# Routed blocks of a mixture-of-experts layer: the high half of the activations turned by DMA in odd blocks

## The reference, cut to what matters

```
logits = x @ router_w ; the 2 best of 8 experts per token, softmax over the two
for each expert e and each token routed to it:
    g, u = split(x @ w1[e])            # 256 -> 2 x 512
    y   += score * (silu(g) * u) @ w2[e]   # 512 -> 256
y += (silu(x @ w_gate) * (x @ w_up)) @ w_down   # shared expert, all tokens
```

## Time and profile before

| | us |
|---|---|
| median of 3 runs (lowest, highest) | 351.46 (351.23, 351.64) |
| span of the profiled execution | 350.0 |
| PE busy in it | 340.2 (97%) |
| DVE, ACT, POOL busy | 235.3 (67%), 214.1 (61%), 197.2 (56%) |
| mean granted PE clock | 0.996 of full |

### The profile page before, as it was taken

How to read it: one execution, slowest core, us unless ns; L and a number is a source line. 1 busy time by engine, 2 the same in 40 slices (tenths; PEclk the granted TensorE clock), 3 DMA queues, 4 the chain that set the end, 5 groups by cost and what they waited for, 6 DMA issues and landing times.

```text
span 350.0 us, 9157 instructions
## 1 busy us (share of the span) xinstructions
PE 340.2 (97%) x2926; PEld 257.0 (73%) x2926; DVE 235.3 (67%) x585; ACT 214.1 (61%) x389; POOL 197.2 (56%) x293
## 2 busy tenths in 40 slices
PE   7999999999999999999999999999999999999994
PEld 7878878888888898888988465656556556666663
DVE  4999989899888887978788554463544543333441
ACT  3678959796877987746536444455545444554452
POOL 4777568786876768565356444353443355344635
PEclk9999999999999999999999999999999999999998
DMA  6992152554875555735765439659677866876761
GB/s 192 391 357 40 33 125 59 125 145 161 198 201 93 151 163 140 214 109 133 250 233 134 108 61 116 92 84 98 80 103 94 95 99 86 98 109 102 88 65 22
DMA packets 76108, 45.90 MB, mean 131 GB/s; under 512 B 59936, under 2 KB 71200, under 8 KB 75680
## 3 DMA queue, kind: packets, MB, share of 16 engines
q1 hardware_dynamic: 62000, 34.82, 41.0%
q0 software_dynamic: 9392, 10.44, 19.4%
q10 hardware_dynamic: 4672, 0.07, 1.2%
HBM read 19.09 MB, written 12.97 MB: 92 GB/s over the span
## 4 chain that ended last, share of the span: by engine, by line
PE 72%; DVE 13%; issue 5%; ACT 4%; DMA 3%; SPq 1%; POOL 1%; DVEq 0%; POOLq 0%; ACTq 0%
PE bU L1124 13%; PE bG L1124 13%; PE bV L1149 7%; PE bQ L1149 6%; PE bU L239 6%; PE bG L239 5%; PE bD L1001 5%; DVE ab L1626 3%; PE bK L1104 3%; PE bV L239 2%; PE bQ L239 2%; DMA xT<-rows 2%; PE bK L239 2%; DVE st L1493 1%; PE bT L891 1%
## 5 line engine op out<-in xcount | busy, mean ns | idle before, releaser
L1626 DVE SCALAR_TENSOR_TENSOR ab<-bU,sg 128x512 f32<-128x512 f32 x64 | 44.1, 689 | 66.3 <-PE bU L1124 52.7
L800 POOL DMA_INDIRECT out_y<-xs,dst_row x32 | 50.6, 1580 | 55.8 <-DMA out_y<-xs,dst_row 26.2
L1278 ACT ACTIVATE sg<-bG 128x512 f32<-128x512 f32 x64 | 38.0, 594 | 43.8 <-PE bG L1124 26.7
L1124 PE MATMUL bG<-we,work 128*128 (+1 forms) x216 | 52.6, 380 | 0.0
L575 POOL DMA_INDIRECT x_rows<-rows,slot_u x32 | 42.0, 1313 | 18.8 <-issue 14.3
L1124 PE MATMUL bU<-we,work 128*128 (+1 forms) x216 | 52.6, 379 | 0.0
L1443 ACT ACTIVATE ws_h<-ab 128x512 f16<-128x512 f32 x36 | 22.7, 630 | 41.5 <-DVE ab L1626 41.5
L1948 DVE TENSOR_TENSOR ws_h<-ab,ws_h 128x512 f16<-128x512 f32 x36 | 24.9, 693 | 20.8 <-ACT ws_h L1443 20.8
L1285 ACT ACTIVATE ah<-ab 128x512 f16<-128x512 f32 x32 | 20.1, 629 | 28.6 <-DVE ab L1626 28.5
L1124 PEld LDWEIGHTS bG<-we,work 128*128 128x128 f16 (+1 forms) x216 | 20.7, 99 | 19.3 <-issue 1.6
L1124 PEld LDWEIGHTS bU<-we,work 128*128 128x128 f16 (+1 forms) x216 | 19.8, 99 | 17.4
(11 more groups left out here) (348 smaller groups left out, 820.0 us busy)
## 6 DMA issues: line engine op xcount, KB each, us to landing
stage<-in_w_expert SPq DMA_DIRECT2D x24, 512.0 KB, 5.0
we<-in_w_shared SPq DMA_DIRECT2D x3, 1024.0 KB, 11.5
out_y<-xs SPq DMA_DIRECT2D x8, 256.0 KB, 2.6
xs<-bo POOLq DMA_DIRECT2D x7, 256.0 KB, 4.6
xs<-in_x SPq DMA_DIRECT2D x1, 1280.0 KB, 18.0
x_rows<-we SPq DMA_DIRECT2D x9, 134.0 KB
xs<-in_x SPq DMA_DIRECT2D x3, 256.0 KB, 4.1
work<-x_rows SPq DMA_TRANSPOSE x40, 2.9
```

The source lines that it names most:

```text
L800: pool.indirect_dma_start(out_rows, bass.IndirectOffsetOnAxis(ap=dst_row[:, b:b + 1], axis=0), ya[b % NY], None, bounds_check=NT * P - 1, ...
L1124: ins = pe.matmul(dst[t * n:(t + 1) * n, :], x2[:, hi * KC + k, t * n:(t + 1) * n], w[t][lo][:, k, half, :], start=s == 0 and k == 0, stop ...
L1278: act.activation(sg[q][:], src[:], ACT.Silu, scale=1.0 / WS).then_inc(S["sg_done"], 1)
L1626: dve.scalar_tensor_tensor(out=ab[q][:], in0=src[:], scalar=1.0 / WS, in1=sg[q][:], op0=ALU.mult, op1=ALU.mult).then_inc(S["a_done"], 1)
```

## The change

In odd blocks up to 33 (17 of the 36 blocks) the high half is no longer turned on PE and copied by ACT: SP issues a transposing DMA for it (`turn_whole`), in the same step and just ahead of the one for the low half, as soon as `ar_h` is written. `expert_down` of an odd block waits for that DMA, and the counts of the semaphores of the remaining PE turns are adapted (`on_pe`). Even blocks and the last two blocks stay as they were. On POOL, the hold counts are read with a load that also asserts their bounds, each to a value of its own, instead of a plain load to one of two registers.

```diff
+        def by_dma(b):
+            return b % 2 == 1 and b < NBLK - 1
+        def on_pe(b):
+            return sum(not by_dma(n) for n in range(b + 1))
+        def high_in(b):
+            return S[f"ath_in{b % NA}"], 16 * sum(by_dma(n) for n in range(b % NA, b + 1, NA))
...
+            def turn_whole(b):
+                n = b % NA
+                sp.wait_ge(S["ah_done"], NP * B + b + 1)
+                if b >= NA:
+                    sp.wait_ge(S["o_ps"], b - NA + 1)
+                sp.dma_start_transpose(aT_h[n], ar_h[n]).then_inc(S[f"ath_in{n}"], 16)
...
             for b in range(NBLK):
+                if by_dma(b):
+                    turn_whole(b)
                 if b < NBLK - 1:
                     turn_low(b)
...
-            hold_reg = [pool.alloc_register(f"hold_reg{q}") for q in range(2)]
-            last_hold_reg = pool.alloc_register("last_hold_reg")
+            hold = {}
...
             def load_hold(b):
                 row = HALF if b - 1 in MIXED else 0
-                pool.reg_load(hold_reg[b % 2], hold_i[row:row + 1, b:b + 1])
+                hold[b] = pool.value_load(hold_i[row:row + 1, b:b + 1], min_val=16, max_val=16 * NBLK)
...
                 if b == NBLK - 2:
-                    pool.reg_load(last_hold_reg, hold_i[0:1, NBLK:NBLK + 1])
+                    hold[NBLK] = pool.value_load(hold_i[0:1, NBLK:NBLK + 1], min_val=16, max_val=16 * NBLK)
...
             def turn_high(b):
                 pe.wait_ge(S["ah_done"], NP * B + b + 1)
                 if b >= 1:
-                    pe.wait_ge(S["ath_done"], b)
+                    pe.wait_ge(S["ath_done"], on_pe(b) - 1)
...
             def expert_down(b, parts=range(3)):
                 n = b % NA
-                pe.wait_ge(S["ath_done"], b + 1)
+                if by_dma(b):
+                    pe.wait_ge(*high_in(b))
+                else:
+                    pe.wait_ge(S["ath_done"], on_pe(b))
...
                 expert_up(b, 0)
-                if b >= 1:
+                if b >= 1 and not by_dma(b - 1):
                     turn_high(b - 1)
                 expert_up(b, 1)
...
                 if b >= NA:
                     act.wait_ge(S["al_done"], NP * B + b - NA + 1)
-                    act.wait_ge(S["ta_ps"], b - NA + 1)
+                    if by_dma(b - NA):
+                        act.wait_ge(*high_in(b - NA))
+                    else:
+                        act.wait_ge(S["ta_ps"], on_pe(b - NA))
                 act.activation(ar_h[n], ab[b % 2][:], ACT.Copy).then_inc(S["ah_done"], 1)
...
                 silu(NP * B + b, b % 2)
-                if b >= 1:
+                if b >= 1 and not by_dma(b - 1):
                     turned_high(b - 1)
```

More of the change, by code:

```diff
@@ L227, in layer_kernel @@
             rt pt slot_const spread_in spread_ps spread_out ends_in ends_ps ends_out tok_in0 tok_in1 end_done padded bexp_done pad_done
-            xg_in0 xg_in1 xg_in2 xg_in3 first_meta0 first_meta1 first_meta2 first_meta3 meta_in0 meta_in1 meta_in2 meta_in3 sign_done score_done dst_done ta_ps ath_done atl_in0 atl_in1 atl_in2 o_ps y_done hold_done row_done lent tl_ps atl_last halves_out scattered0 scattered1""".split()
+            xg_in0 xg_in1 xg_in2 xg_in3 first_meta0 first_meta1 first_meta2 first_meta3 meta_in0 meta_in1 meta_in2 meta_in3 sign_done score_done dst_done ta_ps ath_done atl_in0 atl_in1 atl_in2 o_ps y_done hold_done row_done ath_in0 ath_in1 ath_in2 lent tl_ps atl_last halves_out scattered0 scattered1""".split()
         S = {n: sem(n) for n in names}
@@ L771, in scatter @@
                 if b == NBLK - 1:
-                    pool.wait_ge(S[f"scattered{b % 2}"], pool.snap(last_hold_reg, min_val=16, max_val=16 * NBLK))
+                    pool.wait_ge(S[f"scattered{b % 2}"], hold[NBLK])
                     pool.nop(nofuse=True)
@@ L776, in scatter @@
                 if held(b):
-                    pool.wait_ge(before, pool.snap(hold_reg[b % 2], min_val=16, max_val=16 * NBLK))
+                    pool.wait_ge(before, hold[b])
                 elif b >= 1:
@@ L1446, in turned_high @@
                 n = b % NA
-                act.wait_ge(S["ta_ps"], b + 1)
+                act.wait_ge(S["ta_ps"], on_pe(b))
                 if b >= NA:
```

## The result

The changed kernel takes 358.47 us (median of 4 runs, 357.26 to 362.11), the one before 351.55 in the same session: ratio 1.0205, interval 1.0171 to 1.0239. It is slower by some 7 us where 3.6 were forecast; the sign was right and the time lies in the range, but the size was off by a factor of two.

The account below looks back on a forecast made before the run. PE bounds the loop, and the change makes SP's in-order DMA list short of time: span 350.0 - 3.96 (dropped turns) + 7.6 (PE standing) = 353.6, plus 1.5 to the median = 355.1 us; range 349.0 to 362.0 us.

Parts of the forecast that it names:

- The gain of 3.96 us: PE's chain in the loop: 17 dropped high-half turns, 15 x 0.22 + 2 x 0.33 us, all saved.
- 7.6 us forecast: PE in the loop: standing time, SP's shortfall of 11.4 us less an allowed lag of 3.8 us.
- SP then needs 136.6 us: SP's list, blocks 0 to 31: 114.4 us occupied plus 16 new turns at 1.39 us, 0.10 of it for slow issues.
- (a): SP's list: issue time doesn't bind, the whole 3.96 us are kept, 347.5 us; chance 0.24, whole or in good part.
- SP is short by 11.4 us: SP's list, blocks 0 to 31: SP needs 136.6 us where PE needs 125.2 us.
- SP may lag 3.8 us: Low turn ahead of expert_down's third group: 8.90 us of time less 2.22 to issue and 2.9 to land.
- isn't the tighter: High half's new turn on SP's list: issued ahead of the low one, so not the tighter; no size given.
- The sum 350.0 - 3.96 + 7.6: Whole kernel: profiled span less dropped turns plus PE's standing, 353.6 us of span.
- Blocks 10 and 20: Mixed blocks, stalls ahead of bG: should come first, as 1.7 us of lag are enough.
- the prediction's last sentence: Loop steps: if they get longer with SP still waiting, the DMA engines are the cause, not the list; no size.
- (b): DMA engines: they get crowded and slow issues double to 0.20 us per DMA, about 363 us; chance 0.15.
- (d): High halves wait behind low ones, or POOL's loads decide, 0.9 us on top of any other case; chance 0.01, slower.

Follow-up runs that it names:

- small DMAs: Kernel before with POOL's hold counts loaded with an assertion; SP also issues three tiny plain DMAs in each of 17 odd blocks, PE turns kept: 366.05 us, ratio 1.0388.
- repeated run: The changed kernel measured and profiled once more, no edit, against the kernel before: 358.17 us, ratio 1.0175; its profiled span is 356.6 us.
- first profile: Profiled execution of the changed kernel's first measurement, the longest of its four runs; that measurement's median is 358.47 us, ratio 1.0205.
- asserted loads: Kernel before with only POOL's hold counts loaded with an assertion, as in the change: 351.82 us, ratio 0.9996.
- unused loads: Kernel before with asserted loads, plus three SP register loads nobody reads in odd blocks, absent from the program that ran: 351.94 us, ratio 1.0001, inconclusive.
- bytes alone: Kernel before with asserted loads; in odd blocks ACT issues a plain 128 KB DMA into an unused buffer, SP's list untouched: 352.10 us, ratio 1.0015.
- wider DMA in all blocks: Changed kernel, but one DMA of 1024 columns turns both halves in all blocks but the last, against the kernel before: 354.49 us, ratio 1.0058.

## Why the prediction was right, and where it was not

**What bounds, and the sign: right.** PE's time set the loop, and the change made SP's in-order list, which no busy time shows, a second limit. The small DMAs show that time on this list alone makes PE stand. The price of a turn behind another, taken as 1.29 us, measured 228.43 - 227.15 = 1.28 us on SP's timeline of the changed kernel:

```profile
227.15 1.19 SPq L457 DMA_TRANSPOSE ws_l<-ws_h  x1
228.43 1.22 SPq L449 DMA_TRANSPOSE ws_l<-ws_h  x1
```

**The gain of 3.96 us: supported**, by the run whose added turn is unused (some 3 us slower than the change) and by the 1.9 us that blocks 21 to 33 win where 1.5 were summed.

**How long PE stands: 7.6 us forecast, 8.0 in the repeated run, 9.6 in the first profile.** That 7.6 lies so near is in good part luck. Three steps under that number were wrong, and their errors offset each other.

The first is "SP then needs 136.6 us". SP's waits in the changed kernel, between the low turns of block 0 (197.3) and block 31 (335.8):

```profile
SPq L449 <- DVE ws_h L1975: 11.6, 9, 3.6
SPq L457 <- ACT ws_h L1470: 1.3, 2, 1.2
```

Less the 3.6 us at the start these are 9.3 us, and SP was occupied 138.5 - 9.3 = 129.2 us. The 0.10 us per DMA for slow issues was too much: without it the rows give 128.3 us, the figure of rival (a). With 129.2 in the prediction's one sum SP is short by 4.0 us, the lag takes up 3.8, and PE would hardly stand.

The second is "SP is short by 11.4 us", made over one stretch from block 0 to block 31, with all of SP's waits spent. Waits in a late part can't be spent on an early one. Cut at 290 us, the first part has 8.6 us of waits against 11 x 1.39 + 2.6 = 17.9 us (issues of blocks 1 to 21, and the shortening of PE), short by 9.3 (8.2 with 1.29 us per issue); the second has 9.4 against 6 x 1.39 + 1.3 = 9.6 (blocks 23 to 33), short by 0.2. Most of the loss does lie in the first part: 7.5 of the 8.0 us of standing in the repeated run, and 7.3 of the 9.6 in the first profile, come before 291 us. The forecast, with one sum, had one sign for the whole change. The cut is rough too: up to 290 us SP of the changed kernel still waited 5.3 us.

The third is "SP may lag 3.8 us", worked out with the median landing of 2.9 us. The turns that made PE stand landed after 4.57, 5.43 and 5.22 us in the repeated run, as the chain has them:

```profile
211.31 4.57 DMA ws_l<-ws_h
...
216.10 1.66 PE bQ L1173 x12
...
228.31 5.43 DMA ws_l<-ws_h
...
233.96 1.68 PE bQ L1173 x12
...
243.87 5.22 DMA ws_l<-ws_h
249.13 0.63 PE bV L1173 x8
```

With 4.6 to 5.4 us the lag allowed is 8.90 - 2.22 - 4.6 = 2.1 down to 1.3 us, and 9.3 less that is 7.2 to 8.0 us, near what the runs show. That is worked out afterwards and tests nothing. The formula itself can be tested on single turns. In the first profile the low half of block 31 is ready at 332.73 and is turned 3.06 us later (DVE, SP and PE in the timeline):

```profile
332.01 0.72 DVE L1975 TENSOR_TENSOR ws_h<-ab,ws_h 128x512 f16<-128x512 f32 x1 [0.57 <-ACT ws_h L1470]
...
335.79 1.22 SPq L449 DMA_TRANSPOSE ws_l<-ws_h  x1
...
341.31 0.61 PE L1173 MATMUL bQ<-wd,ws_l 128*128 x4 [1.90 <-DMA ws_l<-ws_h]
342.06 2.74 PE L1145 MATMUL bG<-we,work 128*128 x6
```

It lands 5.48 us after the start of its issue, so the lag allowed is 8.90 - 2.22 - 5.48 = 1.20 us and PE should stand 1.86 us; it stands 1.90. In the repeated run block 29's low turn is 1.91 us late and lands after 5.20 us: 0.43 us expected, 0.45 measured. So the mechanism is right, with each turn's own lag and landing in it; and the late part isn't free once all odd blocks are turned by DMA, though blocks 21 to 33 alone, with up to 2.6 us of lag, stopped nothing.

Long landings aren't the work of the added turns: in profiled runs that add none to SP's list they reach 5.0 us (before), 5.7 (asserted loads), 5.9 (unused loads) and 6.1 (bytes alone), and no PE row waits for them there. What the change added is the lag: 4.28, 2.30 and 3.28 us for the three turns above, each from the end of its input to its issue. The sentence that the high half "isn't the tighter" fell as well: 6.0 of the 8.7 us ahead of bQ in the first profile ended with a high half. By the Trainium skill, VectorE: DVE Perf Modes, "The three transpose paths", the prediction had named another estimate of four turns, 5.24 us; the median landings here, 3.2 and 3.4 us, disagree, but those that stopped PE lay near it.

**The step that failed, and that made the size wrong: products behind a stall, put at nothing.** The sum 350.0 - 3.96 + 7.6 took PE's products at their old durations without giving a reason. The first twelve behind a stall read 1.59 to 1.69 us instead of 1.31, and longer products add 2.4 us in the repeated run and 4.7 in the first profile. Where +3.6 us of span were forecast, they bring the repeated run to +6.4 with the 8.0 us of standing, and the first profile to +10.3 with 9.6. Part of it may be waiting inside a group, which the modelled ends of products count as busy: in the repeated run weight loads into bV waited 3.6 us for low halves. In the first profile two places at half speed, behind the stalls that end at 262.00 and 341.31, are most of the 4.7 us: the twelve products of bG and bU from 263.69 on take 2.62 + 1.66 us instead of 2.58. This goes with a wider spread in that session, 357.26 to 362.11 us against 351.23 to 351.68; the repeated run's four lie within 0.25 us.

**The signs named.** The 76 products, the 19 copies (line 1477) and the 17 DMAs more are there. SP's waits haven't "nearly gone": 9.3 of 14.3 us are left. Blocks 10 and 20 didn't come first: the first long stall is `expert_down` of block 3, and the little idle time ahead of bG is in blocks 5 and 15. By the prediction's last sentence, longer steps with SP still waiting would mean that the DMA engines are the cause. That sign can't tell the two apart: with the small DMAs, which add time on SP's list and next to no bytes, SP still waits 9.7 us up to block 31.

**The rivals.** (a), issue time that doesn't bind, is refuted for the first part of the loop: issues almost without bytes cost 13.7 us, although its price for slow issues was the better one. The Trainium skill, DMA: Bandwidth & Descriptors, "Issuing engines are not separate DMA queues", calls the sequencer's time usually small; here it is 1.2 of some 3 us per turn, and it is what counts. With the change behind block 20 alone, (a) is what happened. (b), crowded DMA engines, gets little support: plain bytes cost little (ratio 1.0015), the same turned bytes with as many issues as before lose nothing (0.9998), and SP's slow issues didn't double but cost less than before. Medians of landing are 3.0 to 3.9 us with added turns and 2.8 to 3.4 without, too close to show a part of (b). (d), POOL's loads, is refuted.

**Open.** Why a few turns land 2 us later than the others, with or without the change. Taking the issue time off SP's list while keeping the turns wasn't tried.

## What to carry to other kernels

An issuing sequencer is a resource with a list and a budget: write down the time of its DMAs per step against the step's length, cut by stage, before anything is added to it. Where it is short, a change can be worth making in a part of the loop only: made up to block 19 alone the same edit cost 1.8%, made from block 21 on alone it gained 0.6%. A transposing DMA cost its issuer nearly the same for 512 and 1024 columns, so turn as many columns as possible with one, as far as what waits for it can wait for the whole; and give what waits for it the slack of a late landing, not of the median.

## What the runs showed of the hardware that was not expected

A turning DMA of 1024 columns occupies SP for 1241 ns, one of 512 columns for 1198; three small plain ones together for 1.85 us. A stall of PE costs more than its length: by the modelled ends, twelve products behind stalls of 2 to 3 us took some 0.3 us longer. In the changed kernel's first profile the granted clock was 0.50, the lower level, from 263.50 to 266.92 and from 342.01 to 345.42, and six products took 2.62 and 2.74 us instead of 1.29. PE had stood 2.63 and 1.90 us just before; behind a stall of 3.34 us in the same run, which ended at 217.22, the clock stayed at the upper level. The profiled runs with the unused turn, the small DMAs, the wider DMA in all blocks and the change from block 9 on have one such place each.

SP's slow issues fall together with instruction fetches. In the profiles of the kernel before, the changed one and its repeat, 22 transposing DMAs behind 196 us keep SP longer than 1.6 us, and 21 of them start within 0.8 us of a 16 KB packet of the instruction queue q8; of all 247 such DMAs, 26 start that near. One such fetch also falls from 213 to 215 us in the changed kernel, while the turn of 211.31 is under way, which lands after 5.68 us (the view charges a packet's whole time to the window in which it starts):

```profile
q1 hardware_dynamic: 518, 0.13, 206.4%
...
q8 instruction: 1, 0.02, 2.9%
```

This is a coincidence in time, and no run tested it. The long landings don't all fall there.
